# Both routings of a two-layer cross-attention and expert block, moved pair by pair into their attentions

## The reference

```python
x = x + tanh(g_xattn[0]) * L0_xattn(layernorm(x), ctx, mask0)   # 16 heads of 16, softmax, wo, bo
x = x + tanh(g_ffn[0])   * L0_ffn(layernorm(x))                 # 8 experts, top 2, capacity 500
x = x + tanh(g_xattn[1]) * L1_xattn(layernorm(x), ctx, mask1)   # 16 heads of 64
x = x + tanh(g_ffn[1])   * L1_ffn(layernorm(x))                 # 8 experts, top 2, no capacity
```

## Time and profile before

| | |
|---|---|
| median of 3 runs | 1683.66 us (1682.76 to 1684.49) |
| profiled execution | 1681.74 us, span 1679.9 us |
| PE, PEld busy | 1311.7 us (78%), 1041.5 us (62%) |
| DVE, ACT, POOL busy | 869.0 (52%), 810.1 (48%), 308.4 us (18%) |
| first attention, one pair of batches | 40 us |
| second attention, one pair | 80 us |

### The profile page before, as it was taken

The page is one execution under the profiler, slowest core; times in us unless marked ns, Lnnn a source line. Parts: engine busy times, 40 slices in busy tenths (PEclk is TensorE's granted clock), DMA queues, the critical chain, the costliest instruction groups (busy, mean ns, idle before and its releaser), DMA issues. The chain is left out here.

```text
span 1679.9 us, 35318 instructions
## 1 busy us (share of the span) xinstructions
PE 1311.7 (78%) x10632; PEld 1041.5 (62%) x10633; DVE 869.0 (52%) x2918; ACT 810.1 (48%) x2219; POOL 308.4 (18%) x337
## 2 busy tenths in 40 slices
PE   3699999984089998059999999999999973049970
PEld 2576676664078888057787878787878753026650
DVE  3466666664035544446665656665665656302223
ACT  3588778773044543136554555555545544013320
POOL 2333333310700000711000000000000000430016
PEclk9899999995589999569999999999999995579995
DMA  5811000000232320220000000000000000822113
GB/s 138 346 29 27 26 26 26 27 2 0 78 139 100 134 104 26 74 83 11 21 11 11 10 10 10 10 10 10 10 10 0 1 1 0 319 60 66 62 58 107
DMA packets 42626, 92.25 MB, mean 55 GB/s; under 512 B 10205, under 2 KB 30877, under 8 KB 39261
## 3 DMA queue, kind: packets, MB, share of 16 engines
q1 hardware_dynamic: 32468, 77.37, 13.6%
q0 software_dynamic: 8192, 13.15, 2.8%
q10 hardware_dynamic: 1872, 0.68, 0.3%
HBM read 66.18 MB, written 24.97 MB: 54 GB/s over the span
## 5 line engine op out<-in xcount | busy, mean ns | idle before, releaser
L507 ACT ACTIVATE b_prob<-b_prob,b_low 100x361 f32<-100x361 f32 x256 | 155.6, 608 | 108.0 <-DVE b_low L596 108.0
L364 PE MATMUL b_ps_p<-b_context_part,b_wk_part 128*128 128x362 f32 x768 | 157.7, 342 | 0.0
L1046 ACT ACTIVATE a_prob<-a_prob,a_low 100x361 f32<-100x361 f32 x256 | 154.2, 605 | 4.4 <-DVE a_low L1164 4.4
L515 ACT COPY b_prob_t<-b_ps_t 128x300 f32<-128x300 f32 x256 | 103.8, 406 | 104.2 <-PE b_ps_t L420 101.3
L370 PE MATMUL b_ps_p<-b_wv_part,b_context_part 128*128 128x512 f32 (+1 forms) x576 | 151.6, 406 | 0.0
L596 DVE CUSTOM_DVE_ANT_0 b_prob<-b_ps_s,b_mask_bias 100x361 f32<-100x361 f32 x256 | 121.3, 532 | 45.3 <-PE b_ps_s L410 30.0
L1164 DVE CUSTOM_DVE_ANT_0 a_prob<-a_ps_s,a_mask_bias 100x361 f32<-100x361 f32 x256 | 121.5, 532 | 34.8 <-PE a_ps_s L947 34.8
L420 PE MATMUL b_ps_t<-ident,b_prob 100*128 100x100 f32 x768 | 117.1, 261 | 22.1 <-ACT b_prob_t L515 21.5
L1054 ACT COPY a_prob_t<-a_ps_t 128x300 f32<-128x300 f32 x256 | 97.7, 409 | 67.7 <-PE a_ps_t L957 64.8
L364 PEld LDWEIGHTS b_ps_p<-b_context_part,b_wk_part 128*128 128x128 f32 x768 | 124.6, 189 | 0.3 <-issue 0.2
L420 PEld LDWEIGHTS b_ps_t<-ident,b_prob 100*128 100x128 f32 x768 | 78.1, 141 | 66.3 <-issue 52.4
(11 more groups left out here) (205 smaller groups left out, 2530.5 us busy)
## 6 DMA issues: line engine op xcount, KB each, us to landing
rows_in<-zero SPq DMA_DIRECT2D x16, 512.0 KB, 13.9
w<-in_c_fc SPq DMA_DIRECT2D x8, 1024.0 KB, 6.3
w<-in_c_proj SPq DMA_DIRECT2D x8, 1024.0 KB, 4.9
f_w<-in_W SPq DMA_DIRECT2D x2, 4096.0 KB
a_context<-in_ctx SPq DMA_DIRECT2D x16, 361.0 KB, 3.6
b_context<-in_ctx SPq DMA_DIRECT2D x16, 361.0 KB
f_xe<-rows_in SPq DMA_DIRECT2D x8, 512.0 KB, 3.9
rows_out<-f_ye SPq DMA_DIRECT2D x8, 512.0 KB, 3.0
```

The lines of the kernel that those rows point to most:

```text
L364: ins = nc.tensor.matmul(bank[:, 0:LN2], w_parts["k"][a][:, k, t * P:(t + 1) * P], cx_parts[s][b][:, k, :], start=m == 0, stop=m == DK * l ...
L507: nc.scalar.activation(prob[0:S, k, 0:L], prob[0:S, k, 0:L], ACT.Exp, bias=low[0:S, k:k + 1], scale=-1.0, accum_out=total[0:S, k:k + 1]).t ...
L515: nc.scalar.copy(pt[:, k % PAIR_PT, :], ps_t[:, 0:KT_N * S]).then_inc(pt_ready.sem, 1)
L1046: nc.scalar.activation(prob[0:S, k, 0:L], prob[0:S, k, 0:L], ACT.Exp, bias=low[0:S, k:k + 1], scale=-1.0, accum_out=total[0:S, r:r + 1]).t ...
```

## The change

A new class `Router` keeps what one pair needs for its normalisation and routing, and both attentions use one. For each pair, one pair late:

- DVE: moments (2 BN_AGGR), the turned rows' copy, the logits' copy, `choose` (2 MAX8, 2 index searches, a cast, 2 or 3 small steps), the counts' copy. In the second attention also `add_z` (gamma, the residual and its sums, for 2 x 256 columns).
- POOL: `scales` (4 small chained steps, one a power), `note` (2 copies), `route` (16 small steps in the first, 12 in the second, nearly all chained), and 4 indirect DMAs (`scatter`). In the second attention also `z_scales` (6 steps, 2 powers).
- ACT: `make_rows` (2 activations of 100 x 256); in the second attention also 2 for z.
- PE: three new units, N (4 transposes of rows), G (4 logits matmuls of 8 columns) and C (2 rank matmuls), each in its own slot.

`normalise(n1_)` and `normalise(n3_)` go, and `feed_forward` becomes `experts_first` and `experts_second` without route, ranks and dispatch. The ranks are kept as a running count on POOL. In the first layer second choices cannot have their final place yet, so each expert has two regions of 512 rows, one for first and one for second choices; ahead of an expert's load SP reads the count of first choices and copies the second choices behind them, a 512 KB transfer from DRAM to DRAM. In the second layer each expert has 14 x 128 rows, and `lay_tiles` (DVE, some 17 small steps) works out which 32 tiles are used. `rows_in` of the first layer is zeroed ahead of the attention by the same number of transfers (16); that of the second by 28 transfers of 512 KB, two behind each context load of the first attention's loop. The last pair routes itself behind its output projection, in slots of its own.

```diff
 def first_schedule(last):
+    at = [[] for _ in range(QUADS + QUAD_VALUE + 5)]
...
+    at[3] += [("K", 1, 1, 0), ("V", 1, 2, 0), ("W", 1, 0, -1)]
+    at[ROUTE_AT + 1].append(("N", 0, 0, -1))
+    at[ROUTE_AT + 2].append(("G", 0, 0, -1))
...
+    at[7] += [("K", 0, 1, 0), ("Q", 0, 1, 0), ("V", 0, 2, 0), ("C", 0, 0, -1)]
```

ROUTE_AT is 4. Before, ("W", 1, 0, -1) stood in slot 4. In the second attention (Z_AT is 3):

```diff
+    for k, kind in enumerate("NGC"):
+        at[Z_AT + 2 + k].append((kind, 0, 0, -1))
```

POOL's program for a pair in the first attention:

```diff
             def steps(i, sched):
+                for p in range(len(sched.slots)):
+                    if sched is full and p == half:
+                        convert(0, i + 2, maxed.at(i, H))
+                    for u, unit in sched.slots[p]:
+                        if unit[0] in ("Q", "K"):
+                            lower(unit, sched.split[u], i, False)
+                    j = routed_pair(i, p)
+                    if j is not None:
+                        router.scales(pool, j)
+                    if sched is full and p == QUADS - 1:
+                        convert(1, i + 2, maxed.at(i, HEADS))
+                    for u, unit in sched.slots[p]:
...
+                        elif unit[0] == "C":
+                            pool.wait_ge(taken.sem, taken.at(i, u + 1))
+                            router.route(pool, i + unit[3])
+                            router.scatter(pool, D_["xs0"])
```

The second experts' weights, on SP in the last pair of the second attention, go into tiles that are dead by then:

```diff
+            sp.wait_ge(unit_done.sem, unit_done.at(last, 0))
+            sp.dma_start(T["wq1"][:, :, :].rearrange("p k w -> p (k w)"), D_["W2"][0, :, :]).then_inc(T["w_late"], 16)
+            sp.wait_ge(unit_done.sem, unit_done.at(last, max(final.find("K", 1) + final.find("V", 1)) + 1))
+            sp.dma_start(T["w1_1"][:, :], D_["W1"]).then_inc(T["w_late"], 16)
+            sp.wait_ge(valued.sem, valued.at(last, H // 2))
+            for f in (1, 2):
+                sp.dma_start(T[f"w2_1_{f}"][:, :], D_["W2"][f, :, :]).then_inc(T["w_late"], 16)
+            sp.wait_ge(scored.sem, scored.at(last, PAIR_STEPS))
...
```

More of the change, by code:

```diff
@@ L327, in _ @@
             convert(1, 1, None)
-            iterations(pool, steps)
+            pool.memset(T["run"][:, :, :, :], 0.0).then_inc(zeroed, 1)
+            pool.wait_ge(zeroed, 8)
+            pool.wait_ge(D_["cleared"][1], D_["cleared_value"][1])
+            for i in range(PAIRS):
+                steps(i, full if i < PAIRS - 1 else final)
+            pool.sem_inc(router.summed, 1)
         @block.tensor
@@ L872, in _ @@
             convert(1, 1, None)
-            iterations(pool, steps)
+            pool.memset(T["run"][:, :, :, :], 0.0).then_inc(zeroed, 1)
+            pool.wait_ge(zeroed, 6)
+            pool.wait_ge(D_["cleared"][0], D_["cleared_value"][0])
+            for i in range(PAIRS):
+                steps(i, full if i < PAIRS - 1 else final)
+            nc.gpsimd.tensor_scalar(T["have"][:, :], T["run"][:, 0, 0, :], float(SLOTS), None, ALU.min).then_inc(zeroed, 1)
+            pool.wait_ge(zeroed, 7)
+            nc.gpsimd.tensor_copy(T["firsts"][:, :], T["have"][:, :]).then_inc(router.summed, 1)
         @block.tensor
@@ L1203, in steps @@
                             find_max(i, FIRST * p + m)
+                    j = routed_pair(i, p)
+                    if j is not None:
+                        dve.wait_ge(taken.sem, taken.at(i, sched.units.index(("W", 1, 0, 0 if p >= QUADS else -1)) + 1))
+                        router.own.begin(j)
+                        router.moments(dve, router.averaged)
                     ended = lagging(p, QUAD_TURN, i)
```

1535 lines of the change are left out of this document (909 added, 626 removed).

## The result

The changed kernel took 1673.68 us (median of 20 runs, 1668.71 to 1694.99) where the kernel before took 1683.41 on the same chip: a ratio of 0.9942 [0.9928, 0.9957], 9.7 us or 0.6% faster. The prediction said 1611 us and 1583 to 1655. The direction was right; seven eighths of the gain are missing. The profiled execution took 1675.58 us, with a span of 1673.8.

A forecast was written before the change was run, and what follows sets the result against it. PE bounds the attentions (96% busy), chains of waits the gaps. Gaps win 55.9 + 74.9 us, attentions pay 28 + 30: 72.8 won from 1681.74 gives 1608.9, with the median's 1.9 us more 1611; range 1583 to 1655.

The forecast's parts named there:

- What the gaps give: Gaps between attention and experts: 55.9 us won in the first and 74.9 in the second, leaving 31.6 and 30.8.
- The 16 route steps of the first tail: Eighth pair's routing on POOL in the first gap: 16 small steps costing 4.2 us.
- The power on POOL: Power steps among POOL's scales: costed like any small chained step at 0.25 us, near the lower bound.
- The wait for the seventh pair's rows in POOL: First gap: the eighth pair waits 3.1 us while POOL still routes the seventh; bounds 0 and 6.
- I take 1.0 us (1.3 start to start) for a scatter inside the attention: POOL in the attentions: a scatter lasts 1.0 us there, as in the quiet gaps; four take 5.2 us.
- scatters alone at 4 us, gives about +10 a pair and 1681: Milder form of the rival that POOL only gets on while DVE pauses (chance 0.06): slow scatters in the attentions.
- The rule weighed against the trace: Skill's 3100 ns for GpSimd-written DMAs beside DVE copies, against 2% in the trace; by the rule 60 us worse.
- I take half of DVE's and ACT's: Attentions: half of DVE's and ACT's added work delays PE; a pair costs 4.1 us in the first, 4.3 in the second.
- The move of W: First attention: moving this unit, an output projection, by one slot lets moments stand in slot 4; costed at nothing.
- POOL is late for the keys: Rival, chance 0.2: POOL's small steps cost 0.5 us, overrunning 1.2 us slack in the first attention; 1642 us.
- The second experts should wait for rows: Second gap: a sign that the expert matmul waits for its rows, not for weights.
- The clears' price of nothing: First attention: 28 clears of 512 KB, 52 GB/s where 28 flowed, were to cost nothing.

The follow-up runs named there:

- f2: Changed kernel with the second batch's output projection back in slot 4 of the first attention, moments behind it, unit N last in slot 5: 1641.66 us.
- e1: Changed kernel without the scatters of the first seven pairs of each attention, rows never reaching their experts: 1626.95 us.
- g1b: Rerun of changed kernel with scatters two and two, projection in slot 4, second attention's choice inside slot 7, unit C ahead of its last value unit: 1613.35 us.
- f2b: Rerun, on a chip with holds, of the changed kernel with the output projection back in slot 4: 1676.14 us.
- c1: The changed kernel, unedited, run again beside three edited kernels on one chip: 1676.02 us.
- e1b: Rerun, beside the unedited change, of the changed kernel without the first seven pairs' scatters in each attention: 1629.15 us.
- e3: Changed kernel with each scatter of a pair waiting until the one before has landed: 1677.37 us.
- c2: The changed kernel, unedited, run again beside the no-scatter, plain-transfer and all-edits kernels: 1670.79 us.
- f1b: Rerun, on a chip with holds, of the changed kernel with a pair's four scatters in two groups of two: 1647.83 us.
- e4: Changed kernel with the first seven pairs' scatters in each attention replaced by plain transfers of the same rows from POOL's queue to fixed rows: 1637.35 us.
- f1: Changed kernel with two scatters issued at once and two in slot 1 of the next pair: 1635.96 us.
- g1: Changed kernel with scatters two and two, projection in slot 4, second attention's choice inside slot 7, unit C ahead of its last value unit: 1610.56 us.
- f3: Changed kernel with the second attention's choice of experts behind slot 7's maxima, nothing else: 1622.73 us.

## Why the prediction was wrong

In its profiled execution the change won 6.1 us where 72.8 were forecast. The 66.7 that are missing are 11.0 in the gaps and 55.7 in the attentions and behind them.

- **What the gaps give: right, a little high.** 119.8 of 130.8 us were won. The parts of the chain stand as forecast; the sizes were short. The 16 route steps of the first tail took 4.4 us (4.2 forecast). The power on POOL lasts 0.73 us (0.80 on average), where I gave every step 0.25, and there are three in the second tail. From the last scatter to the expert matmul it takes 14.3 and 12.0 us, not 11.1 and 9.1. The wait for the seventh pair's rows in POOL was there, 1.81 us, inside the bounds of 0 to 6.
- **"I take 1.0 us (1.3 start to start) for a scatter inside the attention": right in size, and the step that failed.** The scatter takes 1.03 us of POOL. I costed it on POOL alone, set it against POOL's slack, and so put it at nothing in the sum. Its price is that PE's updates stand still while the series is issued, and with them DVE, ACT and PE. Seven pairs' scatters in each attention came to 41.6 us, some 32 of them by the holds. In the sessions without holds it came to less: f2, with all scatters, lies 14.7 us above e1. No row of before could show it, since all 32 scatters of each layer ran while PE had nothing to do; but that is also the reason why the bounds should not have been drawn from those rows alone. The forecast had the right kind of case, "scatters alone at 4 us, gives about +10 a pair and 1681", with another mechanism and a chance that was part of 0.06; that its 1681 lies near the 1674 measured is luck, since the scatters did not last 4 us.
- **The rule weighed against the trace.** The scatters last 1033 ns on average over 32. DVE stood idle through much of the series shown above, so f2, which has no hold, is the better place to look: there 17 scatters of the first attention's 32 have DVE busy nearly all the time and last 1.05 us on average, and six run beside a DVE copy out of PSUM, for 0.26 us of their time, and last 0.99. The Trainium skill (SBUF — State Buffer, "A bandwidth-pool intuition that's wrong (but worth ruling out)") gives some 3100 ns for a DMA whose descriptors GpSimd writes beside a DVE copy. The runs don't show that for this kernel's scatters: DVE doesn't hold them up. No scatter met a copy from SBUF to SBUF, so how one beside such a copy fares isn't shown.
- **"I take half of DVE's and ACT's": right in the mean, wrong in the pieces.** Without scatters a pair of the first attention takes 42.9 us, 2.9 more than before, where I had 4.1. One of the second takes 85.7, 5.6 more, where I had 4.3. Together, seven times each, 20.3 + 39.2 = 59.5 us against 58. In the second the half was too little because of one place: the choice goes in front of slot 7's maxima, which costs 3.5 us of that slot (15.92 against 12.40), the fall of the clock included. In the order of the program this was to be seen; I halved a sum in place of following the one queue that PE waits for. PE's own part was a little high: 2.1 us a pair against the 1.8 and 1.5 of g1b.
- **The move of W, "I cost it at nothing": the working is wrong, the result right.** Slot 3 grows by 1.73 us and slot 4 shrinks by only 0.13. But with W in slot 4 the moments come too late for the rows, and slots 4 and 5 pay as much. f2b and c1 are equal.
- **"POOL is late for the keys": not the cause.** In e1b POOL's whole chain but the scatters stands, and the pair takes 42.9 us; in f2, without holds, the scatters stand too, and it takes 42.9. The steps of the chain measured 0.20 to 0.25 us, 0.28 to 0.33 start to start. Only e3's series of 10 us made this rival true.
- **"The second experts should wait for rows": right.** The clears' price of nothing was not tested, since every kernel has them; e1b moves 75 GB/s in its first attention, about what c2 moves, and a pair takes 42.9 us there.

Added up over the profiled executions, without counting a stretch twice: e1b, the change without the scatters of seven pairs, lies 54.8 us below the kernel before, 18.0 short of the forecast. Its gaps last 32.4 and 36.0 us, 6.1 more than forecast in all; its two attentions take 67 us more than before where I had 58, 9.7 of them in the last pair of the second, whose last projection drains at low clock (5.30 us against 3.67 before); the rest is 3. c2 lies 39.9 above e1b, which is the scatters; 6.6 of this is in the gaps, so part of the 11.0 missing there is theirs. The last 8.8 us are after against c2, two executions of one kernel on two chips. 18.0 + 39.9 + 8.8 = 66.7.

**What stays open.** What holds PE's updates while four indirect transfers are issued, and why it did so in the first measurement and the last three groups, and in no trace of the first two groups, wasn't settled by these runs. The two kinds of session differ in one more thing: in all traces of the first kind some of the engines' semaphore updates have no record (44 in before, 102 in after, 41 in e1b), nearly all of them in series of indirect transfers, the experts' gathers included; in the traces of the second kind 0 or 1 is missing. So the recording itself may take part in the holds, and no run here tells what an execution without recording takes. The pacing of e3 was never run where there are holds. The unedited change was never seen in a session without holds; from f2, which equals it elsewhere, it would take an estimated 1642 us there, still inside the range and above the forecast of 1611.

## What to carry to other kernels

A series of indirect transfers that cost nothing in a quiet gap has to be priced again before it is moved beside a loop that PE bounds: count what waits on PE's signals while it is issued, split the series, and leave room for the buffer that the last of it reads. Small DVE steps put into such a loop belong behind the step that PE waits for next, not in front of it; the share of busy time can't tell these two places apart, the order of the queue can. Where two measurements of nearly the same kernel differ by 30 us, run the unedited kernel beside them before a cause is named.

## What the runs showed that was not expected

- In the first measurement PE's semaphore updates came 2.3 to 4.5 us late in every series of four indirect scatters of 100 rows beside an attention's loop (PE's matmul ended at 243.66, its update came at 247.95), while the recorded ones of DVE, ACT and POOL were on time. Series of two gave at most 2.0 us in f1b and g1b. Four plain transfers in series gave none. The groups e1 to e4 and f1 to g1 show none at all, f1, f2, f3 and g1 with the very files that have holds elsewhere.
- An idle time of PE of 2.73 us (2.50 in the second attention) was followed by 3.4 us at 1.2 GHz, in which the 361-column matmul at 251.35 took 0.97 us in place of 0.47, that line's median. In the second attention a fall of the clock adds about 1.4 us to the slot that it lies in (slot 7 takes 15.9 us where the fall lies in it, and 14.4 where it comes in the slot behind).
- A power of 100x2 on POOL takes 0.73 to 0.80 us, three to four times the 0.20 to 0.25 of a multiplication of that shape. The first scatter of a series starts 0.9 us behind the write of its indices.
